# Two expert passes run as one loop, with the results added to the output rows in DRAM by accumulating scatters

## The chip, the cores and the metric

The kernel runs on one core of a Trainium2 chip. The metric is the device time of one launch in microseconds (us), as the median of several runs. The page and the rows below come from one further execution, taken with the hardware profiler.

## What is computed

One layer of a graph transformer over 6250 nodes with 256 features: a graph attention part, a linear attention ("mix") part over eight heads, and then a feed-forward part with six experts, of which each node uses its two best. Only the last matters here:

```
x = x + gnn(layernorm(x)) + mix(layernorm(x))          # called x2 below
features = layernorm(x)
rh = relu(features @ router_w1 + router_b1)
top_w, top_i = top_k(softmax(rh @ router_w2 + router_b2), 2)
w = softmax(top_w)
h1 = relu(features @ expert_w1[e] + expert_b1[e])       # for the two experts e of a node
h2 = relu(h1 @ expert_w2[e] + expert_b2[e])
y  = h2 @ expert_w3[e] + expert_b3[e]
x = x + w[0] * y(first expert) + w[1] * y(second expert)
```

## The kernel before, in words

The work stands in program order on five engines, each with its own instruction list, joined by semaphores. There are no automatic schedules: an engine does what stands next in its list as soon as its semaphore waits are met. SyncE (SP) issues plain DMAs, GpSimd (POOL) issues the indirect ones. `T` is 50 tiles of 125 nodes, and `PR` 25 pairs of them.

The stages are: the tables of the graph part and the normalised, transposed x; the products of the mix part with the gathers of the graph part; the mixing part; the experts.

**Mixing part** (`PR` steps, some 282 to 400 us). TensorE's `mix(i)` makes the mixed rows of two tiles, VectorE's `mixed_rows(i)` (line 987 of the profile) adds them to x and the graph rows and writes x2 into a ring of four row buffers `xr`, then takes the statistics. TensorE makes router logits, VectorE's `route` picks the two experts, their weights and each node's place in two tables. A row in the ring has `ROW` = 262 numbers: x2 (256), the two numbers of its normalisation, its two weights, its node number and its place in the second table. POOL scatters each tile of such rows into the DRAM table `tab0`, sorted by first expert (line 566). SP meanwhile loads x (`load_x2`, line 357) and the expert weights (line 435).

**Experts.** The table is cut in tiles of 128 rows of one expert each, found at run time; `PAIRS` = 27 pairs of tiles per pass. Pass k = 0 is for first experts, k = 1 for second ones. Within a pass the engines run a software pipeline in `tiles`, one pair a step: in step j TensorE does layer 1 of pair j, layer 2 of j - 1, layer 3 of j - 2 (lines 1333 to 1335; each product as three, of high and low halves) and transposes in between (line 1325); ScalarE copies high halves out of PSUM (`in_h`, `h1_h`, `h2_h`: lines 752, 755, 760), normalises the rows of pair j + 2 (`normal`, line 734) and multiplies the third bias of pair j by its weight (`third_bias`, line 745); VectorE adds biases (line 1116), makes the low halves (lines 1138, 1141, 1146) and, for pair j - 2, weight times layer 3 plus the row (`plus_rows`, line 1125). Each engine loads expert numbers into registers every `EL` = 3 pairs.

- Row buffers `rb` are `U` = 7, each of two tiles of `ROW1` = 518 numbers: a sum of 256 and a `ROW`.
- In pass 0 POOL adds third bias and x2 into the sum (line 577), VectorE adds layer 3, and POOL scatters the whole 518 numbers into `tab1`, sorted by second expert (line 585).
- In pass 1 SP loads rows of `tab1` (line 469), the same is added on top, and POOL scatters the 256 numbers into `out` by node number (line 591).
- Between the passes SP waits for all scatters of pass 0 before it issues the first load of pass 1. Every engine's pipeline ends its pass with j = `PAIRS` + 1 and begins the next with j = -1.
- Rows that fill up a tile have an index above the bound, and the scatter leaves them out.

Of the kernel before, what the change touches and what calls it, by code (L numbers as in the profile page):

```python
# [12 lines left out]
N, D = 6250, 256  # L13
# [34 lines left out]
U = 7  # L48
U1 = 5
# [3 lines left out]
ROW1 = D + ROW  # L53
# [20 lines left out]
def gps_layer(nc, x, src, dst, w_kv, w_q, w_oT, b_out, w_g, a_l, a_r, rw1, rb1, rw2, rb2,  # L74
              ew1, eb1, ew2, eb2, ew3, eb3, out):
    ctx = ExitStack()
    with ctx:
# [11 lines left out]
        def over(name, shape, at, dt=FP32):  # L89
# [7 lines left out]
        tab1 = nc.dram_tensor("tab1", (E * REG + S, ROW1), FP32, kind="Internal").ap()  # L97
# [20 lines left out]
        skip_rows = sb("skip_rows", [128, ROW1])  # L118
        eps_sb = sb("eps_sb", [128, 1])
        arena = sb("arena", [128, U1 * HB * ROW1])  # L120
# [88 lines left out]
        rb = [(arena, weight_in)[u >= U1][:, at:at + HB * ROW1].rearrange("p (b n) -> p b n", b=HB)  # L209
              for u in range(U) for at in (u % U1 * HB * ROW1,)]  # L210
# [11 lines left out]
        b3w = [rows_of(work, HB * F * (2 + b)) for b in range(2)]  # L222
# [62 lines left out]
        sc_out = [sem(f"sc_out{b}") for b in range(RB)]  # L285
# [3 lines left out]
        fill_ready = sem("fill_ready")  # L289
# [6 lines left out]
        l3_done, y_done, b3w_ready, b3w_done = sem("l3_done"), sem("y_done"), sem("b3w_ready"), sem("b3w_done")  # L296
# [4 lines left out]
        al_t = al_tab.rearrange("(p t) n -> p t n", t=T)  # L301
        W1, W2, W3 = 16 * 3, 16 * 7, 16 * 2
# [15 lines left out]
        def experts(engine, regs, k, j):  # L318

            part = regs[(j // EL) % 2]  # L320
            engine.load(part, tab_e[0:1, k, j * HB:(j + EL) * HB])
            return [engine.snap(reg, min_val=0, max_val=E - 1) for reg in part]
# [4 lines left out]
        def tiles(engine, k, regs, step):  # L327


            es = {}  # L330
            for j in range(-1, PAIRS + 2):
                if has(j) and j % EL == 0:
                    for i, e in enumerate(experts(engine, regs, k, j)):
                        es[j + i // HB, i % HB] = e
                step(j, es)
# [4 lines left out]
        def uses(u, n):  # L340
            return (n - u + U - 1) // U

        def has(j):
            return 0 <= j < PAIRS
# [5 lines left out]
        def _(sp):  # L350
# [76 lines left out]
            for i in range(PR):  # L427
                if i + SLOTS < PR:
                    sp.wait_ge(y2_done, i + 1)
                    load_x2(i + SLOTS)  # L430
                if i % 3 == 2 and i // 3 < E:
# [9 lines left out]
            for k in range(2):  # L441
                tab = (tab0, tab1)[k]
                sp.dma_start(tab[E * REG:E * REG + S, :], skip_rows[:, ROW1 - tab.shape[1]:ROW1]).then_inc(fill_out[k], 16)
# [3 lines left out]
            def fill_up(k):  # L447
                tab = (tab0, tab1)[k]
                rows = skip_rows[:, ROW1 - tab.shape[1]:ROW1]
                sp.load(end_regs, fill[0:1, k, 0:E])  # L450
                for reg in end_regs:
                    end = sp.snap(reg, min_val=0, max_val=(E - 1) * REG + N)
                    sp.dma_start(tab[bass.ds(end, S), :], rows).then_inc(fill_out[k], 16)
# [7 lines left out]
            def load(k, j):  # L461

                tab = (tab0, tab1)[k]
                n = k * PAIRS + j
                for h in range(HB):
                    first = sp.value_load(tab_row[0:1, k, j * HB + h:j * HB + h + 1], min_val=0, max_val=E * REG)
                    if h == 0 and turn(n) > 0:
                        sp.wait_ge(z_out[n % U], turn(n) * 16 * HB)
                    sp.dma_start(rb[n % U][:, h, ROW1 - tab.shape[1]:ROW1], tab[bass.ds(first, S), :]).then_inc(r_in[n % U], 16)

            for k in range(2):
                if k == 1:
                    sp.wait_ge(tab_done, 2)
                    for u in range(U):
                        sp.wait_ge(z_out[u], 16 * HB * uses(u, PAIRS))
                    sp.wait_ge(fill_out[1], 16 * (E + 1))
                for j in range(PAIRS):
                    load(k, j)
                    if k == 0 and j == U - 1:
                        fill_up(1)  # L480
            for u in range(U):
                sp.wait_ge(z_out[u], 16 * HB * uses(u, 2 * PAIRS))

        @block.gpsimd
        def _(pool):
# [72 lines left out]
            pool.memset(skip_rows[:, 0:D + C_TOK], 0.0).then_inc(pool_c, 1)  # L558
            pool.iota(skip_rows[:, D + C_TOK:ROW1].bitcast(I32), pattern=[[0, 2]], base=SKIP,
# [10 lines left out]
            for k in range(2):  # L570
                def third_bias(j):

                    n = k * PAIRS + j
                    for h in range(HB):
                        row = rb[n % U][:, h, :]
                        pool.wait_ge(b3w_ready, n * HB + h + 1)
                        pool.tensor_tensor(row[:, 0:D], b3w[n % 2][:, h, :], row[:, D:2 * D] if k == 0 else row[:, 0:D],  # L577
                                           ALU.add).then_inc(b3w_done, 1)

                def scatter(j):  # L580
                    u = (k * PAIRS + j) % U
                    for h in range(HB):
                        pool.wait_ge(y_done, (k * PAIRS + j) * HB + h + 1)
                        if k == 0:
                            pool.indirect_dma_start(
                                out=tab1, out_offset=bass.IndirectOffsetOnAxis(
                                    ap=rb[u][:, h, D + C_POS:D + C_POS + 1].bitcast(I32), axis=0),
                                in_=rb[u][:, h, :], in_offset=None, bounds_check=E * REG - 1, oob_is_err=False
                            ).then_inc(z_out[u], 16)
                        else:  # L590
                            pool.indirect_dma_start(
                                out=out, out_offset=bass.IndirectOffsetOnAxis(
                                    ap=rb[u][:, h, D + C_TOK:D + C_TOK + 1].bitcast(I32), axis=0),
                                in_=rb[u][:, h, 0:D], in_offset=None, bounds_check=N - 1, oob_is_err=False
                            ).then_inc(z_out[u], 16)

                for j in range(PAIRS + 2):
                    if has(j):
                        third_bias(j)
                    if has(j - 2):  # L600
                        scatter(j - 2)
# [3 lines left out]
        def _(act):  # L605
# [121 lines left out]
            for k in range(2):  # L727
                def normal(j):

                    n = k * PAIRS + j  # L730
                    act.wait_ge(r_in[n % U], 16 * HB * (turn(n) + 1))
                    for h in range(HB):
                        row = rb[n % U][:, h, :]
                        act.activation(xe[:, j % 2, h, :], row[:, D:2 * D], ACT.Identity,  # L734
                                       bias=row[:, D + C_NMR:D + C_NMR + 1],
                                       scale=row[:, D + C_R:D + C_R + 1]).then_inc(xe_done, 1)

                def third_bias(j, es):

                    n = k * PAIRS + j  # L740
                    if n >= 2:
                        act.wait_ge(b3w_done, (n - 1) * HB)
                    for h in range(HB):
                        w = D + C_W + k
                        act.activation(b3w[n % 2][:, h, :], b3_sb[:, bass.ds(es[j, h] * D, D)], ACT.Copy,  # L745
                                       scale=rb[n % U][:, h, w:w + 1]).then_inc(b3w_ready, 1)

                def step(j, es):
                    done = k * PAIRS + j + 1
                    if has(j + 1):  # L750
                        act.wait_ge(tin_done, done + 1)
                        act.activation(in_h, tin_ps, ACT.Copy).then_inc(in_h_done, 1)  # L752
                    if has(j):
                        act.wait_ge(th1_done, done)
                        act.activation(h1_h, th1_ps, ACT.Relu).then_inc(h1_h_done, 1)
                    if has(j + 2):
                        normal(j + 2)
                    if has(j - 1):
                        act.wait_ge(th2_done, done - 1)
                        act.activation(h2_h, th2_ps, ACT.Relu).then_inc(h2_h_done, 1)  # L760
                    if has(j):
                        third_bias(j, es)

                normal(0)
                tiles(act, k, act_e, step)
# [3 lines left out]
        def _(dve):  # L769
# [209 lines left out]
            def mixed_rows(i):  # L979
# [5 lines left out]
                if g >= RB and at == 0:  # L985
                    dve.wait_ge(sc_out[g % RB], scattered(g - RB))
# [413 lines left out]
```

## Time and profile before

| | |
|---|---|
| median of 3 runs | 791.03 us |
| lowest and highest | 788.23 and 791.4 us |
| the profiled execution, its own time | 790.04 us |
| span, first to last instruction on the profile | 787.9 us |
| mean granted TensorE clock | 0.938 of full |
| PE busy (matmuls) | 677.1 us, 86% of the span |
| VectorE, ScalarE, POOL busy | 70%, 55%, 51% |
| moved by DMA | 106.24 MB, mean 135 GB/s |

A share of busy time is a mean over stages. What an edit is worth must be read in the stage in which it stands, and there from what the last engine waits for.

### The profile page before, as it was taken

Reading aid. Unit: us, or ns where it says so; the run is one execution under the profiler, and the core shown is the slowest. Engines: PE = TensorE matmul, PEld = TensorE weight load, DVE = VectorE, ACT = ScalarE, POOL = GpSimd, SP = SyncE. Lnnn points to the kernel's source line nnn. Section 1 sums busy time; section 2 is a strip of 40 time slices with the busy share of each in tenths; the row PEclk is TensorE's granted clock in tenths of the full one; section 3 lists DMA queues with packets and bytes.
Section 4 is the critical chain, followed back from the end, with each engine's and each line's share of the span. In section 5 each row is a group of like instructions: output and inputs, shape, how many; then the busy total and the mean of one; then the engine's idle time right before and its main releaser. Section 6 shows DMA issues by size and latency. Waiting matters only on the chain.

```text
span 787.9 us, 15452 instructions
## 1 busy us (share of the span) xinstructions
PE 677.1 (86%) x4744; PEld 624.2 (79%) x4744; DVE 553.3 (70%) x1399; ACT 437.2 (55%) x874; POOL 403.4 (51%) x443
## 2 busy tenths in 40 slices
PE   3878999999999888888860699999993899999992
PEld 2878788888888767777650699999993799999992
DVE  5675678888888766777745377777773477777772
ACT  2636556677777436677730466565651465656551
POOL 3456478877667000454636155556554156565553
PEclk9989999999999989999955799999997699999997
DMA  8875635444443434765324524443433524444420
GB/s 219 190 170 142 167 103 142 132 131 136 128 122 95 157 134 154 240 186 169 111 59 119 169 87 136 143 138 130 141 110 108 148 90 141 139 133 146 124 74 29
DMA packets 72463, 106.24 MB, mean 135 GB/s; under 512 B 24612, under 2 KB 45605, under 8 KB 72386
## 3 DMA queue, kind: packets, MB, share of 16 engines
q1 hardware_dynamic: 51074, 72.57, 32.2%
q0 software_dynamic: 21312, 32.69, 13.6%
q8 instruction: 43, 0.70, 0.4%
q14 instruction: 34, 0.28, 0.1%
HBM read 60.32 MB, written 46.78 MB: 136 GB/s over the span
## 4 chain that ended last, share of the span: by engine, by line
PE 76%; ACT 6%; DMA 4%; DVE 4%; issue 3%; POOL 3%; SPq 1%; POOLq 0%; DVEq 0%; ACTq 0%
PE kv_ps L1333 10%; PE kv_ps L1335 10%; PE kv_ps L1334 10%; PE pt L1325 6%; PE d_ps L1191 5%; PE kv_ps L1168 5%; PE kv_ps L1171 4%; PE kv_ps L1169 4%; PE kv_ps L1268 3%; PE xt_ps L1325 3%; POOL tab L566 2%; ACT staged L708 2%; DMA al_tab<-arena 2%; PE pt L1168 2%; PE pt L1171 2%
## 5 line engine op out<-in xcount | busy, mean ns | idle before, releaser
L1333 PE MATMUL kv_ps<-we_h,now_h 128*128 x648 | 194.2, 300 | 10.7 <-DVE now_l L1138 4.3
L1335 PE MATMUL kv_ps<-we_h,now_l 128*128 x648 | 185.2, 286 | 0.0
L1334 PE MATMUL kv_ps<-we_l,now_h 128*128 x648 | 184.9, 285 | 0.0
L1333 PEld LDWEIGHTS kv_ps<-we_h,now_h 128*128 128x128 f32 x648 | 125.7, 194 | 15.5 <-issue 15.5
L1334 PEld LDWEIGHTS kv_ps<-we_l,now_h 128*128 128x128 f32 x648 | 125.8, 194 | 0.0
L1335 PEld LDWEIGHTS kv_ps<-we_h,now_l 128*128 128x128 f32 x648 | 125.4, 194 | 0.0
L1116 DVE TENSOR_TENSOR work<-kv_ps,be 128x256 f32<-128x256 f32 x216 | 81.9, 419 | 59.6 <-PE kv_ps L1335 57.4
L577 POOL TENSOR_TENSOR arena<-work,arena 128x256 f32<-128x256 f32 x80 | 53.3, 686 | 103.9 <-ACT work L745 103.9
L752 ACT ACTIVATE now_h<-pt 128x512 fp32r<-128x512 f32 x54 | 32.4, 600 | 110.8 <-PE pt L1325 71.9
L537 POOL DMA_INDIRECT alg<-al_tab,src_all x50 | 62.3, 1246 | 39.1 <-issue 25.1
L924 DVE TENSOR_REDUCE ss<-xring 125x16 f32<-125x1040 f32 x50 | 61.7, 1234 | 17.4 <-ACT xring L648 14.3
L540 POOL DMA_INDIRECT arena<-xt_tab,dst_all x50 | 62.2, 1244 | 15.2 <-issue 15.2
L1138 DVE TENSOR_TENSOR now_l<-pt,now_h 128x512 fp32r<-128x512 f32 x54 | 37.3, 692 | 35.1 <-ACT now_h L752 34.2
L1325 PE MATMUL pt<-ident,staged 128*128 128x128 f32 x216 | 34.2, 283 | 32.0 <-ACT staged L734 32.0
L566 POOL DMA_INDIRECT tab<-work,pos x16 | 19.2, 1200 | 77.1 <-DVE work L1052 72.8
L734 ACT ACTIVATE staged<-arena 128x256 f32<-128x256 f32 x80 | 43.5, 597 | 23.3 <-DMA arena<-tab 23.3
L1191 PEld LDWEIGHTS d_ps<-work 125*128 125x128 f32 x400 | 52.1, 191 | 4.9 <-DVE work L938 0.9
L1191 PE MATMUL d_ps<-work 125*128 125x128 f32 x400 | 52.6, 275 | 0.7 <-DVE work L938 0.7
L1325 PEld LDWEIGHTS pt<-ident,staged 128*128 128x128 f32 x216 | 26.2, 145 | 32.2 <-issue 21.0
L1168 PE MATMUL kv_ps<-wkv_h,x_h 128*128 128x512 f32 x120 | 49.8, 415 | 0.6 <-ACT arena L622 0.6
L1169 PE MATMUL kv_ps<-wkv_l,x_h 128*128 128x512 f32 x120 | 47.1, 392 | 0.0
L1268 PE MATMUL kv_ps<-staged,rw_sb 128*128 128x250 f32 x100 | 31.3, 440 | 17.0 <-ACT staged L708 16.4
(239 smaller groups left out, 1825.3 us busy)
## 6 DMA issues: line engine op xcount, KB each, us to landing
arena<-tab SPq DMA_DIRECT2D x40, 259.0 KB
xring<-in_x SPq DMA_DIRECT2D x26, 224.0 KB
xt_tab<-arena SPq DMA_DIRECT2D x10, 568.8 KB
arena<-tab SPq DMA_DIRECT2D x40, 131.0 KB
we_h<-wt_h SPq DMA_DIRECT2D x6, 768.0 KB
we_l<-wt_l SPq DMA_DIRECT2D x6, 768.0 KB
weight_in<-tab SPq DMA_DIRECT2D x14, 259.0 KB
xring<-in_x SPq DMA_DIRECT2D x5, 560.0 KB
```

Source lines behind the costliest of these rows:

```text
L537: pool.indirect_dma_start(out=alg[:, b, t % CH, :], out_offset=None, in_=al_tab, in_offset=bass.IndirectOffsetOnAxis(ap=src_all[:, t:t + 1 ...
L540: pool.indirect_dma_start(out=xtg[:, b, t % CH, :], out_offset=None, in_=xt_tab, in_offset=bass.IndirectOffsetOnAxis(ap=dst_all[:, t:t + 1 ...
L924: dve.reduce_sum(ss[:, t % 2, :], sq[t % 2], axis=AX.X).then_inc(red_done, 1)
L1116: dve.tensor_tensor(rows[:, h, :], outp[:, h, :], be[layer][:, bass.ds(es[j, h] * F, F)], ALU.add).then_inc(finished, 1)
L1168: pe.matmul(outp, x_h[:, t, c, :], w_h(c), start=c == 0, stop=False)
L1169: pe.matmul(outp, x_h[:, t, c, :], w_l(c), start=False, stop=False)
L1191: last = pe.matmul(d_ps[:, at], vs[t % VB][:, at], ks[t % VB][:, at], start=False, stop=t == T - 1, skip_group_check=True)
L1268: last = pe.matmul(rh_ps[:, 0:2 * P], rw1_sb[:, c, :], xTr[:, :, c, 0:P], start=c == 0, stop=c == KC - 1)
L1325: last = pe.transpose(outp[:, h, c, :], rows[:, h, c * 128:(c + 1) * 128], ident[:, :])
L1333: pe.matmul(outp, hi[:, c, :], we_h[:, w], start=c == 0, stop=False)
L1334: pe.matmul(outp, hi[:, c, :], we_l[:, w], start=False, stop=False)
L1335: last = pe.matmul(outp, lo[:, c, :], we_h[:, w], start=False, stop=c == KC - 1)
```

## The change

- There is one loop over `ALL` = 54 pairs n; pass k is n // `PAIRS`. The software pipeline no longer ends and begins between the passes.
- In the mixing part SP also stores each pair of tiles of x2 from the ring to `out` (6.4 MB in 25 steps of two DMAs), after a wait on `x2_done`.
- A row buffer holds one `ROW` per row, and there are ten. Table `tab1` has rows of 262 numbers as `tab0` has.
- POOL copies the rows of pass 0 into `tab1` as they were loaded, `AHEAD` = 5 pairs ahead of the pair whose results it scatters (`second_rows`). The addition of line 577 is gone.
- ScalarE writes weight times third bias to one of `YB` = 4 buffers `yw`, VectorE adds weight times layer 3 to it (`weighted`), and POOL scatters it with `compute_op=ALU.add` onto `out` in DRAM (`add_rows`), in both passes.
- SP waits for the copies of pass 0 before the first load of pass 1; POOL waits for the last ten adds of pass 0 before the first add of pass 1.

```diff
-U = 7
-U1 = 5
+U = 10
-ROW1 = D + ROW
+ALL = 2 * PAIRS
+AHEAD = 5
+YB = 4
...
-        b3w = [rows_of(work, HB * F * (2 + b)) for b in range(2)]
+        yw = [rows_of(work, HB * F * (2 + b)) for b in range(YB)]
...
-            for j in range(-1, PAIRS + 2):
+            for n in range(-1, ALL + 2):
...
+        def added(n):
+            return z_out[n % U], 16 * HB * (turn(n) + 1)
+        def copied(n):
+            return second_out[n % U], 16 * HB * (turn(n) + 1)
... SP, mixing part, in each step i behind load_x2(i + SLOTS)
+                sp.wait_ge(x2_done, i + 1)
+                wide(out_t[:, 2 * i:2 * i + 2, :], xr[g % RB][:, at:at + 2, 0:D], x2_out[g % RB])
... SP, experts
-            sp.wait_ge(tab_done, 1)
+            sp.wait_ge(tab_done, 2)
             sp.wait_ge(fill_out[0], 16 * (E + 1))
             for g in range(GROUPS - RB, GROUPS):
                 sp.wait_ge(sc_out[g % RB], scattered(g))
-            for k in range(2):
-                if k == 1:
-                    sp.wait_ge(tab_done, 2)
-                    for u in range(U):
-                        sp.wait_ge(z_out[u], 16 * HB * uses(u, PAIRS))
-                    sp.wait_ge(fill_out[1], 16 * (E + 1))
-                for j in range(PAIRS):
-                    load(k, j)
+                sp.wait_ge(x2_out[g % RB], stored(g))
+            for n in range(ALL):
+                k, j = n // PAIRS, n % PAIRS
+                for h in range(HB):
+                    first = sp.value_load(tab_row[0:1, k, j * HB + h:j * HB + h + 1], min_val=0, max_val=E * REG)
+                    if h == 0 and n >= U:
+                        sp.wait_ge(*added(n - U))
+                        if n - U < PAIRS:
+                            sp.wait_ge(*copied(n - U))
+                    if n == PAIRS and h == 0:
+                        sp.wait_ge(fill_out[1], 16 * (E + 1))
+                        for m in range(PAIRS - U, PAIRS):
+                            sp.wait_ge(*copied(m))
+                    sp.dma_start(rb[n % U][:, h, :], (tab0, tab1)[k][bass.ds(first, S), :]).then_inc(r_in[n % U], 16)
... POOL, experts (third_bias and scatter of before are gone)
+            def second_rows(n):
+                u = n % U
+                pool.wait_ge(r_in[u], 16 * HB * (turn(n) + 1))
+                for h in range(HB):
+                    pool.indirect_dma_start(
+                        out=tab1, out_offset=bass.IndirectOffsetOnAxis(
+                            ap=rb[u][:, h, C_POS:C_POS + 1].bitcast(I32), axis=0),
+                        in_=rb[u][:, h, :], in_offset=None, bounds_check=E * REG - 1, oob_is_err=False
+                    ).then_inc(second_out[u], 16)
+            def add_rows(n):
+                u = n % U
+                for h in range(HB):
+                    pool.wait_ge(y_done, n * HB + h + 1)
+                    pool.indirect_dma_start(
+                        out=out, out_offset=bass.IndirectOffsetOnAxis(
+                            ap=rb[u][:, h, C_TOK:C_TOK + 1].bitcast(I32), axis=0),
+                        in_=yw[n % YB][:, h, :], in_offset=None, bounds_check=N - 1, oob_is_err=False, compute_op=ALU.add
+                    ).then_inc(z_out[u], 16)
+            for n in range(AHEAD):
+                second_rows(n)
+            for g in range(GROUPS - RB, GROUPS):
+                pool.wait_ge(x2_out[g % RB], stored(g))
+            for n in range(ALL):
+                if n == PAIRS:
+                    for m in range(PAIRS - U, PAIRS):
+                        pool.wait_ge(*added(m))
+                add_rows(n)
+                if n + AHEAD < PAIRS:
+                    second_rows(n + AHEAD)
... ScalarE
+                if n >= YB:
+                    act.wait_ge(*added(n - YB))
+                    act.activation(yw[n % YB][:, h, :], b3_sb[:, bass.ds(es[n, h] * D, D)], ACT.Copy,
+                                   scale=rb[n % U][:, h, w:w + 1]).then_inc(b3w_ready, 1)
... VectorE, mixing part, at the first step of groups 4 and 5
                     dve.wait_ge(sc_out[g % RB], scattered(g - RB))
+                    dve.wait_ge(x2_out[g % RB], stored(g - RB))
... VectorE, experts (weighted, in the place of plus_rows)
+                dve.wait_ge(b3w_ready, (n + 1) * HB)
+                    dve.scalar_tensor_tensor(yw[n % YB][:, h, :], l3_ps[n % 2][:, h, :], rb[n % U][:, h, w:w + 1], yw[n % YB][:, h, :],
+                                             ALU.mult, ALU.add).then_inc(y_done, 1)
```

## Rows read from the trace of the kernel before

**Rows 1.** The page's first part: busy us, share of the span, instructions.

```profile
PE 677.1 (86%) x4744; PEld 624.2 (79%) x4744; DVE 553.3 (70%) x1399; ACT 437.2 (55%) x874; POOL 403.4 (51%) x443
```

**Rows 2.** Busy time by stretch: PE, PEld, DVE, ACT, POOL, PEclk, DMA share, GB/s.

```profile
282.00:400.00 118.00, 98.13 (x644) 85.73 (x644) 82.00 (x331) 77.15 (x144) 43.18 (x36) 0.93 0.54 170
...
340.00:360.00 20.00, 16.81 (x122) 15.01 (x122) 14.93 (x59) 13.57 (x26) 11.95 (x10) 1.00 0.76 234
...
460.00:480.00 20.00, 20.00 (x173) 20.00 (x172) 15.83 (x33) 13.25 (x28) 10.99 (x14) 1.00 0.39 132
...
594.00:620.00 26.00, 11.55 (x63) 9.73 (x62) 6.54 (x13) 5.76 (x12) 7.21 (x8) 0.65 0.51 147
620.00:769.00 149.00, 147.15 (x1236) 145.75 (x1236) 110.98 (x231) 87.69 (x179) 82.01 (x100) 0.99 0.40 118
```

**Rows 3.** The chain that ended last, between the passes: start, us, what.

```profile
598.35 0.98 POOL tab L585
...
602.65 2.06 DMA tab<-weight_in
...
605.65 0.34 SPq L469
...
606.76 3.12 DMA weight_in<-tab
```

**Rows 4.** Timeline of ScalarE: start us, us, engine, line, operation, tiles.

```profile
446.17 0.90 ACT L745 ACTIVATE work<-xring,arena 128x256 f32 x2
...
540.91 1.08 ACT L734 ACTIVATE staged<-weight_in 128x256 f32<-128x256 f32 x2
542.25 0.60 ACT L760 ACTIVATE now_h<-xt_ps 128x512 fp32r<-128x512 f32 x1 [0.25 <-PE xt_ps L1325]
542.74 0.90 ACT L745 ACTIVATE work<-xring,arena 128x256 f32 x2
...
548.36 0.90 ACT L745 ACTIVATE work<-xring,arena 128x256 f32 x2
...
588.52 0.90 ACT L745 ACTIVATE work<-xring,arena 128x256 f32 x2
...
620.18 0.89 ACT L745 ACTIVATE work<-xring,weight_in 128x256 f32 x2
...
626.53 0.91 ACT L745 ACTIVATE work<-xring,arena 128x256 f32 x2
```

**Rows 5.** Timeline of VectorE in a steady step, and TensorE near the boundary.

```profile
542.02 0.88 DVE L1125 SCALAR_TENSOR_TENSOR arena<-kv_ps,arena 128x256 f32<-128x256 f32 x2 [0.15 <-PE kv_ps L1335]
...
591.05 0.36 PE L1333 MATMUL kv_ps<-we_h,now_h 128*128 x1
```

**Rows 6.** POOL's groups: count, busy us, mean ns, idle before and its releaser.

```profile
L537 POOL DMA_INDIRECT alg<-al_tab,src_all x50 | 62.3, 1246 | 39.1 <-issue 25.1 <-DVE arena L901 14.0
...
L577 POOL TENSOR_TENSOR arena<-work,arena 128x256 f32<-128x256 f32 x80 | 53.3, 686 | 103.9 <-ACT work L745 103.9
L585 POOL DMA_INDIRECT tab<-arena x40 | 39.5, 988 | 9.3 <-issue 8.9 <-DVE arena L1125 0.3
L591 POOL DMA_INDIRECT out_x<-arena x40 | 39.5, 987 | 9.9 <-issue 9.3 <-DVE arena L1125 0.3
L566 POOL DMA_INDIRECT tab<-arena,pos x24 | 28.6, 1192 | 23.9 <-DVE arena L1052 17.2 <-issue 6.7
```

**Rows 7.** Timeline of VectorE, POOL and SP before the first expert load.

```profile
427.64 0.18 DVE L1105 CAST tab_e<-gsum_sb 1x54 int32<-1x54 f32 x1
427.71 1.19 POOL L566 DMA_INDIRECT tab<-arena,pos  x1 [0.30 <-issue]
...
432.41 10.37 SPq L469 DMA_DIRECT2D arena<-tab  x10
```

**Rows 8.** Timeline of POOL, its last instruction.

```profile
777.78 0.98 POOL L591 DMA_INDIRECT out_x<-arena  x1 [0.30 <-issue]
```

**Rows 9.** The page's DMA queues: packets, MB, share of 16 engines' span.

```profile
q0 software_dynamic: 21312, 32.69, 13.6%
```

More of the change, by code:

```diff
@@ L206, in gps_layer @@
         fill = sb("fill", [1, 2, EP], I32)
-        rb = [(arena, weight_in)[u >= U1][:, at:at + HB * ROW1].rearrange("p (b n) -> p b n", b=HB)
-              for u in range(U) for at in (u % U1 * HB * ROW1,)]
+        rb = [arena[:, u * HB * ROW:(u + 1) * HB * ROW].rearrange("p (b n) -> p b n", b=HB) for u in range(U)]
         WT = HB * KC * S
@@ L301, in gps_layer @@
         al_t = al_tab.rearrange("(p t) n -> p t n", t=T)
+        out_t = out.rearrange("(p t) n -> p t n", t=T)
         W1, W2, W3 = 16 * 3, 16 * 7, 16 * 2
@@ L316, in scattered, with stored, experts @@
             return 16 * sum(2 * SIZES[a] for a in range(g % RB, g + 1, RB))
-        def experts(engine, regs, k, j):
-            part = regs[(j // EL) % 2]
+        def stored(g):
+            return 32 * sum(SIZES[a] for a in range(g % RB, g + 1, RB))
+        def experts(engine, regs, n):
+            k, j = n // PAIRS, n % PAIRS
+            part = regs[(n // EL) % 2]
             engine.load(part, tab_e[0:1, k, j * HB:(j + EL) * HB])
@@ L448, in fill_up @@
                 tab = (tab0, tab1)[k]
-                rows = skip_rows[:, ROW1 - tab.shape[1]:ROW1]
                 sp.load(end_regs, fill[0:1, k, 0:E])
@@ L567, in _ @@
                                             in_=xr[g % RB][:, j, :], in_offset=None).then_inc(sc_out[g % RB], 16)
[L570 to L601, printed above, removed]
@@ L726, in _ @@
             act.wait_ge(b3_in, 16)
[L727 to L765, printed above, removed]
@@ new lines, in normal, with third_bias @@
+            def normal(n):
+                act.wait_ge(r_in[n % U], 16 * HB * (turn(n) + 1))
+                for h in range(HB):
+                    row = rb[n % U][:, h, :]
+                    act.activation(xe[:, n % 2, h, :], row[:, 0:D], ACT.Identity,
+                                   bias=row[:, C_NMR:C_NMR + 1], scale=row[:, C_R:C_R + 1]).then_inc(xe_done, 1)
+            def third_bias(n, es):
+                if n >= YB:
+                    act.wait_ge(*added(n - YB))
+                for h in range(HB):
+                    w = C_W + n // PAIRS
+                    act.activation(yw[n % YB][:, h, :], b3_sb[:, bass.ds(es[n, h] * D, D)], ACT.Copy,
+                                   scale=rb[n % U][:, h, w:w + 1]).then_inc(b3w_ready, 1)
@@ new lines, in step @@
+            def step(n, es):
+                if has(n + 1):
+                    act.wait_ge(tin_done, n + 2)
+                    act.activation(in_h, tin_ps, ACT.Copy).then_inc(in_h_done, 1)
+                if has(n):
+                    act.wait_ge(th1_done, n + 1)
+                    act.activation(h1_h, th1_ps, ACT.Relu).then_inc(h1_h_done, 1)
+                if has(n + 2):
+                    normal(n + 2)
+                if has(n - 1):
+                    act.wait_ge(th2_done, n)
+                    act.activation(h2_h, th2_ps, ACT.Relu).then_inc(h2_h_done, 1)
+                if has(n):
+                    third_bias(n, es)
@@ L768, in _ @@
+            normal(0)
+            tiles(act, act_e, step)
         @block.vector
@@ new lines, in plus_bias, with weighted @@
+            def plus_bias(rows, outp, layer, n, es, finished):
+                for h in range(HB):
+                    dve.tensor_tensor(rows[:, h, :], outp[:, h, :], be[layer][:, bass.ds(es[n, h] * F, F)], ALU.add).then_inc(finished, 1)
+            def weighted(n):
+                dve.wait_ge(l3_done, n + 1)
+                dve.wait_ge(b3w_ready, (n + 1) * HB)
+                for h in range(HB):
+                    w = C_W + n // PAIRS
+                    dve.scalar_tensor_tensor(yw[n % YB][:, h, :], l3_ps[n % 2][:, h, :], rb[n % U][:, h, w:w + 1], yw[n % YB][:, h, :],
+                                             ALU.mult, ALU.add).then_inc(y_done, 1)
@@ new lines, in step @@
+            def step(n, es):
+                if has(n):
+                    dve.wait_ge(l1_done, n + 1)
+                    plus_bias(hs1, l1_ps, 0, n, es, hs1_done)
+                if has(n - 1):
+                    dve.wait_ge(l2_done, n)
+                    plus_bias(hs2, l2_ps, 1, n - 1, es, hs2_done)
+                if has(n + 1):
+                    dve.wait_ge(in_h_done, n + 2)
+                    dve.tensor_tensor(in_l, tin_ps, in_h.bitcast(FP32), ALU.subtract).then_inc(in_l_done, 1)
+                if has(n):
+                    dve.wait_ge(h1_h_done, n + 1)
+                    dve.scalar_tensor_tensor(h1_l, th1_ps, 0.0, h1_h.bitcast(FP32), ALU.max, ALU.subtract).then_inc(h1_l_done, 1)
+                if has(n - 2):
+                    weighted(n - 2)
+                if has(n - 1):
+                    dve.wait_ge(h2_h_done, n)
+                    dve.scalar_tensor_tensor(h2_l, th2_ps, 0.0, h2_h.bitcast(FP32), ALU.max, ALU.subtract).then_inc(h2_l_done, 1)
@@ L1151, in _ @@
+            tiles(dve, dve_e, step)
         @block.tensor
@@ new lines, in step @@
+            def step(n, es):
+                if has(n):
+                    pe.wait_ge(in_l_done, n + 1)
+                    for h in range(HB):
+                        last = expert_layer(l1_ps[:, h, :], 0, in_h[:, h, :, :], in_l[:, h, :, :], es[n, h])
+                    last.then_inc(l1_done, 1)
+                if has(n - 1):
+                    pe.wait_ge(h1_l_done, n)
+                    for h in range(HB):
+                        last = expert_layer(l2_ps[:, h, :], 1, h1_h[:, h, :, :], h1_l[:, h, :, :], es[n - 1, h])
+                    last.then_inc(l2_done, 1)
+                if has(n + 1):
+                    pe.wait_ge(xe_done, (n + 2) * HB)
+                    turned(tin_ps, xe[:, (n + 1) % 2, :, :]).then_inc(tin_done, 1)
+                if has(n):
+                    pe.wait_ge(hs1_done, (n + 1) * HB)
+                    turned(th1_ps, hs1).then_inc(th1_done, 1)
+                if has(n - 2):
+                    m = n - 2
+                    pe.wait_ge(h2_l_done, m + 1)
+                    if m >= 2:
+                        pe.wait_ge(y_done, (m - 1) * HB)
+                    for h in range(HB):
+                        last = expert_layer(l3_ps[m % 2][:, h, :], 2, h2_h[:, h, :, :], h2_l[:, h, :, :], es[m, h])
+                    last.then_inc(l3_done, 1)
+                if has(n - 1):
+                    pe.wait_ge(hs2_done, n * HB)
+                    turned(th2_ps, hs2).then_inc(th2_done, 1)
@@ L1373 @@
+            tiles(pe, pe_e, step)
 def kernel(**inputs):
```

116 lines of the change are left out of this document (24 added, 92 removed).

## The prediction

> **What bounds the kernel now.** I read the page's first part to see which engine is the fullest: TensorE, with 677.1 us of 787.9 [rows 1]. That alone says nothing of a change that removes no matmul. So I read the busy time by stretch. Inside a pass TensorE is the bound without a gap: 20.00 of 20 us at full clock, with DVE at 79%, ACT at 66%, POOL at 55% and the DMA engines at 0.39 of their time. The stretch between the passes is another matter: 11.55 us busy of 26, at a mean clock of 0.65 [rows 2]. The chain of waits says what fills it: POOL issues the last six scatters of pass 0 (0.98 us each), the last takes 2.06 us to land, SP then reads the tile's place and issues a load at 605.65, and the second half of the pair, on its way at 606.76, lands after 3.12 us. Only then can ScalarE normalise pair 27 [rows 3]. Before the drain the pipeline empties step by step, and behind it fills again at half clock.
>
> The one clock in all passes is ScalarE's `third_bias`, once a step. Two neighbours stand 548.36 - 542.74 = 5.62 us apart: the length of a step where TensorE binds. That of pair 25 starts at 588.52, that of pair 27, the first of pass 1, at 620.18, that of pair 28 at 626.53 [rows 4].
>
> **What is removed.** In one loop pair 27 is two steps behind pair 25: 588.52 + 2 x 5.62 = 599.76 in place of 620.18, so 20.42 us less. The next step took 6.35 us, because matmuls still ran at the lower of TensorE's two levels (1.2 GHz; the engine had idled before); in a loop that doesn't stop it takes 5.62, 0.73 us less. From there on the steps are what they were. Together 21.15 us. The registers are loaded every three pairs as before, and 27 is a multiple of three. From pair 0 to pair 25 the mean step was (588.52 - 446.17) / 25 = 5.69 us [rows 4], so some steps are longer; this stays.
>
> **POOL in pass 0.** Removed are two additions of 0.69 us a pair; added are two scatters, so that POOL now issues four a pair for the first 22 pairs. A scatter of 128 rows takes 0.99 us whether a row has 2 KB (line 585) or 1 KB (line 591) [rows 6], with 0.30 us of issue before it [rows 8]: 1.29. The two copies: 2.58 us. The two adds are of a kind the trace does not show. Lower bound: a plain scatter, 1.29 us; I see no reason for less. Upper bound from rows: the dearest indirect DMA, the gather of line 537, 1.25 + 0.30 = 1.55. The sum is 5.16 to 5.68 us a pair against a mean step of 5.69. POOL keeps up, but with nothing left at the upper end; from 1.55 us an add it becomes the bound. I take the lower value, since the same line with the same rows is the nearest, and cost it at nothing; TensorE's 5.62 us hides it. If that cover is gone, each 0.1 us of an add costs 22 x 0.2 = 4.4 us. In pass 1 POOL has 2.6 to 3.1 us of work in 5.62. The first five copies, 13 us, begin once pair 0 is loaded, 4.2 us behind 432.41 [rows 7], and end near 450; the first result comes two steps behind 446.17, so they delay nothing.
>
> **The wait on the copies.** The last copy, of pair 26, stands behind the adds of pair 21. VectorE's line 1125 for pair m starts 542.74 - 542.02 = 0.72 us before ScalarE's line 745 of pair m + 2 [rows 4, 5]. So for pair 21 it starts at 588.52 - 2 x 5.62 - 0.72 = 576.56; the first half is done at 577.0. Four issues of 1.29 us follow, the last starts at about 581.0 and lands as the one at 602.65 did, seen by SP in some 2.3 us: 583.3. Issue to landing of a pair's loads took 606.76 + 3.12 - 605.65 = 4.23 us [rows 3]. With 0.2 us for eleven more semaphores the rows of pair 27 are there at 587.7. ScalarE wants them 542.74 - 540.91 = 1.83 us before line 745 of pair 25: 586.69. So `normal(27)` is 1.0 us late. Behind it on ScalarE stands `h2_h` of pair 24 (line 760), which then starts near 588.8 in place of 588.0; VectorE's low half behind it ends some 0.8 us later, near 590.2. TensorE begins layer 3 of pair 24 at 591.05 [rows 5]. It is hidden, by less than 1 us. If POOL runs late by x, TensorE pays x less 0.8 us once: 0 with the adds at 1.29 us, about 1 with two of 1.55 and steps of 5.62. For this thin cover I take 0.4 us.
>
> **The other new waits.** POOL waits before the adds of pair 27 for those of pair 26. They start a step, 5.62 us, earlier, take 2.6 us to issue and 2.3 - 1.3 = 1 us more to land: hidden, unless an add lands over 2 us later than a plain scatter. ScalarE waits before the third bias of pair n for the adds of pair n - 4. These can start at line 745 of n - 2, less 0.3 us, so 11.5 us earlier, and need 3.6 us plus the lag behind one pair of copies, 2.6 us: hidden by 5 us. Behind this wait stands the next step's `in_h`, for which TensorE waits. Cost 0.
>
> **DMA engines.** The software queue's 21312 packets took 13.6% of the engines' 787.9 us [rows 9], which is 0.136 x 16 x 787.9 / 21312 = 0.080 us a packet. A pair adds 256 rows, 16 for each engine. Pass 0 has 0.39 x 5.62 = 2.2 us a pair of engine time now [rows 2]; the copies are half as long as the scatters that they replace, and the adds come on top: 16 x 0.08 = 1.3 us if an add is a plain write. That is a share of 0.62. From (5.62 - 2.2) / 16 = 0.21 us a row the engines would be the bound.
>
> The Trainium skill bears on this: its page "Collectives: The Full Stack", in Part 3 under "Why ReduceScatter is half of AllGather", says that an add in the DMA path costs no cycles of its own but needs two source reads on one ring, and so runs at half the rate of a copy. No row here shows an add. By that rule, as an estimate, a row would take 0.16 us and a pair 2.6 us, a share of 0.85, still under the step.
>
> **Stores in the mixing part.** 25 times 2 DMAs store 6250 rows of 1 KB: 6250 / 16 x 0.08 = 31 us of engine time over 118 us, on top of a share of 0.54: 0.81. In the fullest 20 us, with 0.76 and 234 GB/s, another 0.27 makes 1.03 [rows 2]: here the queues back up by a microsecond or so. SP issues 4 DMAs a step in place of 2, at 0.34 us [rows 3], under 1.5 us of a step of 118 / 25 = 4.7 us. The loads of x are five steps ahead, and x2 is made in the same step as what SP waited for before, so `load_x2` comes no more than part of a step later. VectorE's new wait is for a store four groups old. Cost 0; upper bound 4 us, a step lost.
>
> **Start and end.** The first load waits for the last scatter at 427.71 and goes at 432.41 [rows 7]; the stores have long landed, and the second list of tiles, for which SP now waits as well, is written at 427.82, before that scatter lands. Five more semaphores: 0.2 us. The end: the last scatter starts at 777.78 [rows 8], then it lands. An add reads and writes the row: lower bound 0, upper bound another 2.3 us. I take 1.0.
>
> **The sum** against the profiled execution: 790.04 - 21.15 + 0.4 + 0.2 + 1.0 = 770.5. The median of the runs is 1.0 above this execution: 771.5 us.
>
> **The rivals.**
>
> *A. Forecast: the gap goes, and all that is new is hidden.* 768 to 775, with the terms at 0 to their upper ends. Chance 0.71.
>
> *B. POOL is the bound of pass 0.* An add costs more than 1.55 us. For it: the price isn't shown and POOL is at 92% even with the cheapest. Against: 128 rows cost the same at 1 and 2 KB. At 1.75 us: 22 x 0.4 - 0.8 = 8 us, so 779.5. Range 775 to 788. Chance 0.12.
>
> *C. The stores or the adds crowd the mixing part or the boundary.* The share of 1.03 in one stretch speaks for it, the distance of five steps against. One or two steps of 4.7 us lost: 776 to 781. Chance 0.08.
>
> *D. Slower: the adds take the DMA engines.* Place: both passes, all 54 pairs; ScalarE's wait for `yw` passes it to TensorE. The step is then 2.2 + 16p for a price p a row. It decides from p = 0.24 us, three times a plain packet: 54 x (2.2 + 3.84 - 5.62) = 23 us, all that is gained. At 0.26 it is 40 us, so 811. For it: no row shows a read and a write of DRAM in one packet. Against: the factor of three. Chance 0.09, of which 0.02 lies within 0.5% of before.
>
> The Trainium skill's "DMA: Bandwidth & Descriptors", under "Two DMAs through the same engine are not ordered", says that descriptors on an engine are pipelined, read-modify-writes too. No row here shows it; it speaks against D.
>
> **How the numbers follow.** 0.5% (4 us) is about what a measurement of this kernel can tell from no change: the three runs span 3.2 us. Faster than 787 are A, C and nearly all of B: 0.90. Within 4 us: 0.03, what is left of B and 0.02 of D. Slower: 0.07 of D. The range must leave out no more than 0.2: from 766 (A's end less the runs' spread) to 783 it leaves out D, the upper part of B and a little below, some 0.15. A's own range is 768 to 775.
>
> **What would show it.** Right: no stretch between passes with TensorE idle for over 2 us, clock 1.00 from pair 1 to the end; line 745's successor at 5.62 us steps through pair 27; POOL some 92% busy with issue in pass 0; the indirect adds near 1.0 us each. Wrong: ScalarE idle before the third bias with a DMA as releaser (D), VectorE's results long done when POOL issues their add, and steps of 6 us for the first 22 pairs only (B); steps over 4.7 us in the mixing part (C).

## The result: 0.5% faster, not 2.5%

The changed kernel takes 785.78 us (median of 13 runs, 783.38 to 787.92), the one before 789.97 us in the same comparison (13 runs, 786.74 to 792.05). The ratio is 0.9951, 95% interval 0.9937 to 0.9965. The prediction was 771.5 us, 766 to 783.

The page of the changed kernel, first part:

```profile
PE 675.1 (86%) x4744; PEld 621.8 (79%) x4744; DVE 550.6 (70%) x1399; ACT 436.9 (56%) x874; POOL 448.2 (57%) x389
```

TensorE's work is what it was [rows 1]. POOL's went from 403 to 448 us, though 54 instructions fewer stand on its line. Its groups:

```profile
L596 POOL DMA_INDIRECT out_x<-work,arena x108 | 169.0, 1564 | 99.0 <-DVE work L1130 75.1 <-issue 23.9
...
L585 POOL DMA_INDIRECT tab<-arena x54 | 54.9, 1016 | 23.8 <-issue 14.3 <-DMA arena<-tab 7.6 <-DVE work L1130 1.8
```

A copy takes 1.02 us, near the 0.99 of the scatters of 128 rows before [rows 6]. A scatter that adds takes 1.56. Two of each, with 0.30 us of issue, are one pair of pass 0, as the timeline of POOL there shows:

```profile
562.45 1.58 POOL L596 DMA_INDIRECT out_x<-work,arena  x1 [0.30 <-issue]
564.33 1.58 POOL L596 DMA_INDIRECT out_x<-work,arena  x1 [0.30 <-issue]
566.21 1.04 POOL L585 DMA_INDIRECT tab<-arena  x1 [0.30 <-issue]
567.55 1.01 POOL L585 DMA_INDIRECT tab<-arena  x1 [0.30 <-issue]
568.87 1.58 POOL L596 DMA_INDIRECT out_x<-work,arena  x1 [0.30 <-issue]
```

From 562.45 to 568.87 are 6.42 us, and POOL waits for nobody in them: it is the bound, against TensorE's 5.62. The busy time by stretch shows the same from the side (PE, PEld, DVE, ACT, POOL, PEclk, DMA share, GB/s):

```profile
282.00:400.00 118.00, 97.30 (x644) 85.17 (x644) 84.60 (x340) 77.95 (x146) 43.13 (x36) 0.94 0.72 216
...
480.00:520.00 40.00, 39.64 (x338) 39.17 (x336) 30.06 (x64) 24.13 (x50) 32.39 (x26) 1.00 0.67 127
...
560.00:600.00 40.00, 35.84 (x295) 34.38 (x293) 23.93 (x52) 18.87 (x39) 32.39 (x26) 1.00 0.54 93
...
640.00:680.00 40.00, 39.66 (x340) 39.43 (x338) 30.32 (x64) 24.26 (x51) 21.74 (x14) 1.00 0.56 89
```

POOL is busy for 32.39 of 40 us early in pass 0 and late in it; with the issue gaps that is all of its time. Early in the pass TensorE still runs at 39.64 of 40, because there are four `yw` buffers to lag behind in. Late in it TensorE is down to 35.84. In pass 1, without copies, it is full again. ScalarE's timeline tells where the lag is paid (line 752 is `third_bias`, line 743 `normal`; the bracket is the idle time before and what ended it):

```profile
449.05 0.90 ACT L752 ACTIVATE work<-xring,arena 128x256 f32 x2
...
568.16 0.91 ACT L752 ACTIVATE work<-xring,arena 128x256 f32 x2 [3.02 <-DMA out_x<-work,arena]
...
593.98 0.91 ACT L752 ACTIVATE work<-xring,arena 128x256 f32 x2 [2.39 <-DMA out_x<-work,arena]
...
605.76 1.09 ACT L743 ACTIVATE staged<-arena 128x256 f32<-128x256 f32 x2 [9.91 <-DMA arena<-tab]
607.24 0.90 ACT L752 ACTIVATE work<-xring,arena 128x256 f32 x2
...
618.89 0.90 ACT L752 ACTIVATE work<-xring,arena 128x256 f32 x2
...
766.65 0.90 ACT L752 ACTIVATE work<-xring,arena 128x256 f32 x2
```

There are two kinds of wait. From pair 13 to pair 24 ScalarE waits for an add to land before it may write `yw` again (568.16 is pair 20, 593.98 pair 24), and steps take 6.4 us. Before `normal(27)` it waits 9.91 us for the first rows of pass 1. The chain of waits says why they are late:

```profile
598.32 1.04 POOL tab L585
...
599.67 2.09 DMA tab<-arena
602.00 0.34 SPq L488
...
603.10 2.64 DMA arena<-tab
...
606.27 0.58 ACT staged L743
```

POOL begins the last copy at 599.67, and SP may issue the load once it has landed. The copy stands behind 22 pairs of adds on POOL, and so carries the lag that they have built up.

**Where the time went**, by `third_bias`, line 745 before [rows 4] and 752 after, in the two profiled executions (790.04 and 785.97 us):

| stretch | before | after | difference |
|---|---|---|---|
| start to pair 0 | 446.17 | 449.05 | +2.9 |
| pair 0 to 24 (before: 582.90 - 446.17) | 136.73 | 144.93 | +8.2 |
| pair 24 to 25 | 5.62 | 13.26 | +7.6 |
| pair 25 to 27 | 31.66 | 11.65 | -20.0 |
| pair 27 to 53 (before: to 768.89) | 148.71 | 147.76 | -1.0 |
| pair 53 to the end | 21.15 | 19.32 | -1.8 |
| sum | | | -4.1 |

The gap went, as forecast: 21.0 us, the -20.0 and the -1.0 of the table. POOL took 15.8 us of it back, half in longer steps and half at the boundary. The lag that is to be expected from the timeline, for the 22 pairs with copies and against the mean step of 5.69 us before, is 22 x (6.42 - 5.69) = 16.1 us.

### The profile page after: what moved, and what is told of

It is laid out like the page before. It is cut to its first block, busy times and chain, and to the rows that moved or that the text cites. A ratio compares the mean times of both kernels' runs of the same rounds, so it can differ in the third digit from the quotient of the medians.

```text
span 783.8 us, 15543 instructions
## 1 busy us (share of the span) xinstructions
PE 675.1 (86%) x4744; PEld 621.8 (79%) x4744; DVE 550.6 (70%) x1399; ACT 436.9 (56%) x874; POOL 448.2 (57%) x389
## 3 DMA queue, kind: packets, MB, share of 16 engines
q0 software_dynamic: 32544, 32.70, 24.4%
## 4 chain that ended last, share of the span: by engine, by line
PE 68%; POOL 7%; ACT 6%; issue 6%; DMA 6%; DVE 5%; SPq 1%; ACTq 0%; POOLq 0%; DVEq 0%
PE kv_ps L1337 8%; PE kv_ps L1338 7%; PE kv_ps L1339 7%; PE d_ps L1195 5%; PE kv_ps L1172 5%; PE pt L1329 5%; PE kv_ps L1175 5%; PE kv_ps L1173 5%; PE kv_ps L1272 3%; POOL out_x L596 3%; PE xt_ps L1329 2%; POOL tab L576 2%; PE pt L1263 2%; ACT staged L719 2%; PE pt L1175 2%
## 5 line engine op out<-in xcount | busy, mean ns | idle before, releaser
L596 POOL DMA_INDIRECT out_x<-work,arena x108 | 169.0, 1564 | 99.0 <-DVE work L1130 75.1
L743 ACT ACTIVATE staged<-arena 128x256 f32<-128x256 f32 x108 | 58.7, 597 | 33.3 <-DMA arena<-tab 33.3
L930 DVE TENSOR_REDUCE ss<-xring 125x16 f32<-125x1040 f32 x50 | 61.7, 1234 | 17.1 <-ACT xring L659 15.9
L585 POOL DMA_INDIRECT tab<-arena x54 | 54.9, 1016 | 23.8 <-issue 14.3
L752 ACT ACTIVATE work<-xring,arena 128x256 f32 x108 | 48.6, 500 | 28.6 <-DMA out_x<-work,arena 28.6
L1150 DVE SCALAR_TENSOR_TENSOR now_l<-xt_ps,now_h 128x512 fp32r<-128x512 f32 x54 | 37.3, 690 | 18.8 <-ACT now_h L766 18.7
```

Of the source, the lines that this page charges most:

```text
L596: pool.indirect_dma_start(out=out, out_offset=bass.IndirectOffsetOnAxis(ap=rb[u][:, h, C_TOK:C_TOK + 1].bitcast(I32), axis=0), in_=yw[n % ...
L743: act.activation(xe[:, n % 2, h, :], row[:, 0:D], ACT.Identity, bias=row[:, C_NMR:C_NMR + 1], scale=row[:, C_R:C_R + 1]).then_inc(xe_done, 1)
L930: dve.reduce_sum(ss[:, t % 2, :], sq[t % 2], axis=AX.X).then_inc(red_done, 1)
```

## The experiments

Theory P: POOL's time for an adding scatter, 1.56 us and 0.30 of issue, is what ate the gain. Rival D: it is the DMA engines' work for an add. Rival S: it is the stores of x2, or the DMA load in general. Ratios are to the kernel before, measured beside each: 790.88 us beside the two kernels with plain scatters, the one with copies eight pairs ahead alone and the one with both, 791.72 us beside the other four.

### Plain scatters in the place of adding ones

```diff
-                        in_=yw[n % YB][:, h, :], in_offset=None, bounds_check=N - 1, oob_is_err=False, compute_op=ALU.add
+                        in_=yw[n % YB][:, h, :], in_offset=None, bounds_check=N - 1, oob_is_err=False
```

> The changed kernel with plain scatters in the place of the adding ones: the rows of out then hold one pass's term, not the sum. Everything else, waits too, stays. Theory P (POOL's issue time is the bound of pass 0: an adding scatter takes 1.56 us and 0.30 us of issue, a pair with two copies 6.4 us against TensorE's 5.62): a plain one takes 0.99 us, a pair 5.2 us, so pass 0 runs at TensorE's step, the wait before pair 27 goes, and the time is 786 - 8 - 7.5 = 770 us. Rival S (the stores of x2 in the mixing part and the copies crowd the DMA engines): little moves, 783 us or more. Rival D (the DMA engines' work of an add, not POOL's): also 770 us here; the next run tells it from P.

Measured: 768.96 us, ratio 0.9723 (0.9685 to 0.9761). The group of the scatter, and the busy time by stretch in pass 0 and pass 1:

```profile
L596 POOL DMA_INDIRECT out_x<-work,arena x108 | 105.9, 981 | 144.2 <-DVE work L1130 126.9 <-issue 17.3
```

```profile
480.00:520.00 40.00, 39.85 (x341) 39.60 (x341) 30.48 (x65) 24.45 (x51) 27.49 (x29) 1.00 0.47 139
640.00:680.00 40.00, 39.97 (x342) 39.74 (x341) 30.63 (x65) 24.57 (x51) 13.73 (x14) 1.00 0.30 93
```

One flag on the instruction is worth 2.3% (0.9951 to 0.9723), or 17 to 18 us. Rival S falls: stores and copies are all still there. What is left between P and D is whose time an add takes. The DMA share fell as well, from 0.67 to 0.47 and from 0.56 to 0.30, so this run can't say.

### Plain scatters and POOL time without DMA

```diff
                     pool.wait_ge(y_done, n * HB + h + 1)
+                    if n or h:
+                        pool.wait_ge(spare_done, n * HB + h)
+                    pool.tensor_tensor(weight_in[:, 0:200], b3_sb[:, 0:200], b3_sb[:, 0:200], ALU.add).then_inc(spare_done, 1)
                     pool.indirect_dma_start(
...
-                        in_=yw[n % YB][:, h, :], in_offset=None, bounds_check=N - 1, oob_is_err=False, compute_op=ALU.add
+                        in_=yw[n % YB][:, h, :], in_offset=None, bounds_check=N - 1, oob_is_err=False
...
             for n in range(AHEAD):
                 second_rows(n)
+            pool.wait_ge(b3_in, 16)
```

> As the run with plain scatters, with one addition of 128 x 200 numbers on POOL before each of the 108 scatters into out, which adds some 0.6 us of POOL time to each and nothing to the DMA engines. The rows of out hold one pass's term. Theory P: the steps of pass 0 are at 6.3 to 6.5 us again, with ScalarE waiting for yw or for the rows of pair 27, and the time is 783 to 787 us. Rival D (it is the DMA engines' time for an add that counts): 770 to 772 us as with plain scatters alone.

Measured: 778.97 us, ratio 0.9851 (0.9817 to 0.9885): 10 us above plain scatters alone, where D expects none. P's size was missed too: it expected 783 to 787 us. The trace gives a reason: the addition takes 0.53 us, but the scatter behind it starts 0.17 us later and not 0.30, so it adds some 0.4 us and not 0.6, less than the 0.58 us by which an adding scatter is dearer. From POOL's timeline:

```profile
549.78 0.54 POOL L599 TENSOR_TENSOR weight_in<-xring 128x200 f32<-128x200 f32 x1
550.49 0.99 POOL L600 DMA_INDIRECT out_x<-work,arena  x1 [0.17 <-POOL weight_in L599]
...
553.49 0.97 POOL L586 DMA_INDIRECT tab<-arena  x1 [0.30 <-issue]
...
555.75 0.55 POOL L599 TENSOR_TENSOR weight_in<-xring 128x200 f32<-128x200 f32 x1
```

A pair takes 555.75 - 549.78 = 5.97 us. The lag over 22 pairs, 22 x (5.97 - 5.69) = 6 us, hardly reaches ScalarE's wait for `yw` and is met at the boundary:

```profile
586.14 0.91 ACT L757 ACTIVATE work<-xring,arena 128x256 f32 x2 [0.33 <-DMA out_x<-work,arena]
598.18 0.90 ACT L757 ACTIVATE work<-xring,arena 128x256 f32 x2
```

The step from pair 24 to 25 took 598.18 - 586.14 = 12.04 us, 6.4 over 5.62. Of the 9.8 us between this trace and that of plain scatters alone, 6.9 lie between pairs 24 and 27. Another 2.4 lie between pairs 0 and 24, 1.6 of them in the first step; the trace shows no cause for these. So POOL's time alone, with the DMA engines at their load of plain scatters, brings a loss at the boundary back. The longer steps before it this run does not show: its lag was too small for them.

### Copies eight pairs ahead

```diff
-AHEAD = 5
+AHEAD = 8
```

> The changed kernel with the copies 8 pairs ahead (AHEAD = 8) in the place of 5. POOL issues three pairs more of copies in its idle time before the first result, and the last copy stands behind the adds of pair 18. Theory P with four yw buffers: the long wait before pair 27 (7.6 us) goes; pass 0 still falls back to POOL's 6.4 us a step once its lag is over some 5 us, for about 19 x 0.73 - 5 = 9 us in all; 786 - 7.6 = 778 us. Rival (the wait at the boundary comes from the loads or from the fill rows, not from POOL's lag): 784 to 786 us.

Measured: 776.51 us, ratio 0.9827 (0.9792 to 0.9862). No step at the boundary is long any more: `third_bias` of pair 23 is at 587.91, that of pair 25 at 597.13. ScalarE's wait for `yw` stays, up to pair 24, as one line of the waits says (total us, times, longest):

```profile
ACT work L752 <- DMA out_x<-work,arena: 29.2, 13, 3.3
```

### Eight buffers for the results

```diff
-YB = 4
+YB = 8
...
-        yw = [rows_of(work, HB * F * (2 + b)) for b in range(YB)]
+        yw = [rows_of(work, HB * F * (2 + b)) for b in range(4)] + [rows_of(weight_in, HB * F * b) for b in range(YB - 4)]
```

> The changed kernel with eight yw buffers in the place of four, and the copies 5 pairs ahead as it has them. Theory P: ScalarE no longer waits for yw, so the steps of pass 0 stay at 5.6 us, but POOL's lag of 22 x (6.4 - 5.7) = 16 us is then met whole at the boundary, where the copy of pair 26 stands behind the adds of pair 21: a step of some 20 us there and 784 to 787 us in all, no gain. Rival (yw is what costs, the boundary a thing apart): 778 us.

Measured: 787.54 us, ratio 0.9946 (0.9926 to 0.9966), the same as the changed kernel. From pair 2 to pair 24 steps take 5.6 to 6.3 us; then ScalarE waits 17.35 us for the rows of pair 27:

```profile
584.53 0.90 ACT L752 ACTIVATE work<-xring,arena 128x256 f32 x2
...
605.79 1.09 ACT L743 ACTIVATE staged<-arena 128x256 f32<-128x256 f32 x2 [17.35 <-DMA arena<-tab]
606.78 0.57 ACT L766 ACTIVATE now_h<-xt_ps 128x512 fp32r<-128x512 f32 x1
607.26 0.89 ACT L752 ACTIVATE work<-xring,arena 128x256 f32 x2
```

The step of 607.26 - 584.53 = 22.73 us is 17.1 over a plain one. That is P's lag in one piece, where the changed kernel pays 8.2 and 7.6. To take away the earlier of two waits for the same lag gives nothing, for the later one meets it whole. To take away the later one, as the run before did, gave 9 us (785.78 to 776.51), its own 7.6 and little more.

### Both

> The copies 8 pairs ahead and eight yw buffers in the place of four (four more in memory that is free by then). Theory P: POOL may now lag by up to four pairs more with its adds and catches up once the copies are out, 1.9 us a pair; neither ScalarE's wait for yw nor the wait before pair 27 binds; pass 0 runs at 5.6 to 5.7 us a step and the time is 770 to 772 us. Rival D (DMA engines): the work for them is the same as in the changed kernel, so pass 0 stays near 6.4 us a step and the time over 778 us.

The edit is that of the last two together. Measured: 769.60 us, ratio 0.9729 (0.9696 to 0.9762). The adding scatters take 1.56 us as before, and the DMA share in pass 0 is still high (0.63 from 435 to 590 us); but now POOL lags only with work that nobody waits for, and catches up in the last pairs of pass 0, when the copies are out. Its timeline:

```profile
583.22 1.58 POOL L596 DMA_INDIRECT out_x<-work,arena  x1 [0.30 <-issue]
585.11 1.58 POOL L596 DMA_INDIRECT out_x<-work,arena  x1 [0.30 <-issue]
586.99 1.57 POOL L596 DMA_INDIRECT out_x<-weight_in,arena  x1 [0.30 <-DVE weight_in L1130]
588.86 1.55 POOL L596 DMA_INDIRECT out_x<-weight_in,arena  x1 [0.30 <-issue]
```

And ScalarE's, `third_bias` of pairs 27 and 28:

```profile
604.40 0.90 ACT L752 ACTIVATE work<-xring,arena 128x256 f32 x2
610.02 0.90 ACT L752 ACTIVATE weight_in<-xring,arena 128x256 f32 x2
```

This rules D out: the same adds and the same copies, and no step between pairs 23 and 28 is over 6.2 us. It is the fastest version here that still adds, 2.7% below the kernel before, and as fast as the one with plain scatters. The two constants make a table:

| | `YB` = 4 | `YB` = 8 |
|---|---|---|
| `AHEAD` = 5 | 0.9951 | 0.9946 |
| `AHEAD` = 8 | 0.9827 | 0.9729 |

### No stores in the mixing part

```diff
-                sp.wait_ge(x2_done, i + 1)
-                wide(out_t[:, 2 * i:2 * i + 2, :], xr[g % RB][:, at:at + 2, 0:D], x2_out[g % RB])
...
-                sp.wait_ge(x2_out[g % RB], stored(g))
...
-            for g in range(GROUPS - RB, GROUPS):
-                pool.wait_ge(x2_out[g % RB], stored(g))
...
-                    dve.wait_ge(x2_out[g % RB], stored(g - RB))
```

> The changed kernel without the stores of x2 into out in the mixing part, and without the waits on them: the adds go onto whatever out holds, so x2 is missing from the result. The traces show the mixing part's steps where they were before, so the stores are hidden: 784 to 786 us and the mixing part as long as with them. Rival S (the stores cost some 3 us, the amount by which the first third bias comes later than before): 782 to 783 us, and the first third bias near 446 us.

Measured: 787.83 us, ratio 0.9937 (0.9916 to 0.9958). The interval overlaps that of the changed kernel (0.9937 to 0.9965), so the stores cost at most some 3 us, and the runs show no cost. In the trace the part from the first to the last row sum of the graph rows takes 395.46 - 275.36 = 120.1 us without them; with them it took 390.65 - 274.83 = 115.8, and before the change 387.86 - 272.07 = 115.8. This profiled execution was the longest of its five (792.19 us), so its first third bias, at 453.65, says little on the start; the medians decide against S.

### Adding scatters of 64 rows

```diff
-                            ap=rb[u][:, h, C_TOK:C_TOK + 1].bitcast(I32), axis=0),
-                        in_=yw[n % YB][:, h, :], in_offset=None, ...
+                            ap=rb[u][0:64, h, C_TOK:C_TOK + 1].bitcast(I32), axis=0),
+                        in_=yw[n % YB][0:64, h, :], in_offset=None, ...
```

> The changed kernel with adding scatters of the first 64 rows of each tile alone: half of the rows get no expert term. It measures what POOL's 1.56 us for an adding scatter of 128 rows consists of. If the price goes by rows, an add takes 0.8 to 1.0 us, POOL is under TensorE's step and the time is 770 to 772 us. If it is mostly fixed, it takes over 1.3 us and the time stays at 780 us or more.

Measured: 782.06 us, one run. The group:

```profile
L596 POOL DMA_INDIRECT out_x<-work,arena x108 | 154.1, 1427 | 108.5 <-DVE work L1130 82.6 <-issue 25.9
```

Half of the rows make it 0.14 us cheaper, 1.43 in place of 1.56. Between 64 and 128 rows the price hardly moves; where POOL binds in pass 0, steps took 6.1 to 6.3 us. By these two sizes, cutting such scatters in pieces would cost and skipping empty rows would save little; neither was run.

### The kernel before, once more

> The kernel before once more, for a second trace. In the trace shown its first third bias starts at 446.2 us, and in five traces of kernels with the change at 448.3 to 450.0, though the code ahead of the mixing part is the same. If that is chance of the executions, this one can lie anywhere from 446 to 450; if it belongs to the change, it is near 446 again.

Measured: 792.00 us. The first third bias, and the two on both sides of the gap:

```profile
449.61 0.50 ACT L745 ACTIVATE work<-xring,arena 128x256 f32 x1
...
597.22 0.90 ACT L745 ACTIVATE work<-xring,weight_in 128x256 f32 x2
...
623.58 0.90 ACT L745 ACTIVATE work<-xring,weight_in 128x256 f32 x2
```

It starts 3.4 us later than in the first trace of the same kernel. So the +2.9 us in the table of stretches is no more than the difference between two executions of one kernel. The parts that matter hold against this trace too: from pair 0 to 25 the changed kernel is 15.8 us longer, and from pair 25 to 53 it is 19.3 us shorter, in place of 21.0.

## Why the prediction was wrong

- **The gap.** Forecast -21.15 us, measured -21.0 (pair 25 to 53), or -19.3 against the second trace of the kernel before. Right in place and size.
- **The step that failed: POOL in pass 0.** The prediction bounded an adding scatter by rows between 1.29 and 1.55 us with its issue, took the lower value "since the same line with the same rows is the nearest", and cost it at nothing. It is 1.56 + 0.30 = 1.86 to 1.88 us, above both ends. The upper end was the dearest indirect DMA in the trace, and no row held one that reads its destination; the page can't bound an operation that it doesn't show by what it does. The text had the rule for it: 4.4 us for each 0.1 us of an add. Its own rival B, with 1.87 put in: 22 x 2 x (1.87 - 1.55) - 0.8 = 13.3, so 784.8 us, against 785.78. The mechanism was among the rivals, with a chance of 0.12. The term that was mis-sized is the price of an adding scatter, 1.29 us where it is 1.87; with POOL at 92% of a step by the lowest price, rival B deserved a larger chance.
- **The wait on the copies.** Costed at 0.4 us with under 1 us of cover; it took 7.6. The working was right ("if POOL runs late by x, TensorE pays x less 0.8 us"), x was not. That the lag has a second outlet, the wait for `yw`, the prediction took for 5 us of cover; it holds for half of the pass, and then carries the other 8.2 us.
- **DMA engines.** They cost no time, as forecast, but their prices were wrong. In pass 1 the software queue (packets, MB, share of the 16 engines) carries the scatters into `out` alone. These are 120 us with 43 plain ones (plain scatters, 620 to 740 us) and 120 us with 42 adding ones (the changed kernel, 635 to 755 us):

```profile
q0 software_dynamic: 2064, 5.32, 12.4%
...
q0 software_dynamic: 6131, 5.27, 40.2%
```

A plain scatter of 128 rows is 48 packets, so the prediction's 0.080 us a packet was not the price of a row. A plain row took 0.124 x 16 x 120 / (43 x 128) = 0.043 us of an engine, an added one 0.402 x 16 x 120 / (42 x 128) = 0.144. The sum reckoned with 0.08, and rival D needed 0.24. Against D the prediction held "the factor of three", yet an added row did cost 3.3 times a plain one. D failed because plain rows are cheap: with plain scatters the share in pass 0 was 0.47, where the prediction's sum gave 0.62, and with adds it was 0.67. The Trainium skill's page "Collectives: The Full Stack" (Part 3, "Why ReduceScatter is half of AllGather") gives half the rate of a copy for the reduce of a collective. This trace does not agree for an adding scatter, 3.3 times and not twice; the prediction's estimate of 0.16 us comes near 0.144 only by its plain row of 0.08.
- **Stores in the mixing part.** Costed at nothing, with a share of 0.81; the share is 0.72 where it was 0.54 [rows 2], and the runs show no cost.
- **The barrier before the adds of pair 27.** Hidden, as forecast: from pair 27 on the steps of the changed kernel take 5.6 to 6.2 us, and POOL, which begins the first add of pair 27 at 630.54, waited 2.29 us before it for VectorE's result and not for an add.
- **Start and end.** +0.2 was lost among differences of 3 us. The end was forecast 1.0 us longer and is 1.8 us shorter.

## What to carry to other kernels

An operation that the trace doesn't show is not safely bounded by its relatives, and this matters most when its engine is at 92% of a step: give that engine's lag a price in microseconds per 0.1 us of the unknown, and let the range reach it. A lag on an in-order engine is paid wherever somebody waits for that engine, so count all the waits behind it. Removing the earlier of two moved its loss to the later (0.9946 for 0.9951), removing the later gave back little more than its own part (0.9827), removing both gave all of it back (0.9729). On such an engine, put what the next phase waits for (here the copies) early into its idle time, and give the rest buffers enough to be late.

## What was not expected of the hardware

- A scatter that adds in DRAM takes POOL 1.56 us for 128 rows of 1 KB, against 0.98 us for a plain one; 1.43 us for 64 rows. In the changed kernel all 108 took between 1.55 and 1.60 us, early and late, at DMA shares of 0.67 and of 0.56. Why so little of the price goes by rows isn't shown.
- A plain scatter of 128 rows of 1 KB leaves 48 packets in the trace, an adding one 96 more (the software queue has 22176 packets with plain scatters and 32544 in the changed kernel, over 108 scatters), and a row takes the DMA engines 0.043 and 0.144 us.
- POOL's issue gap is 0.30 us between two indirect DMAs but 0.17 us behind an addition.
- The span ends 9.1 us after POOL's last plain scatter (777.78 + 0.98 to 787.9) and 5.5 us after its last adding one (776.74 + 1.55 to 783.8). The other traces bear this out: 5.6 to 5.8 us behind adding scatters of 128 rows, 8.5 behind plain ones and behind adding ones of 64 rows. The traces show nothing in that stretch, and its cause is open.
- Two traces of the same kernel differ by 3.4 us ahead of the experts, nearly as much as the change gained: a single pair of traces must be compared stretch by stretch.
